# A fused attention and expert stage on Trainium2: a fifth place for the tanh arguments, and TensorE's side work cut and spread

## What is computed

```
def _L3_attn_ref(x, W1, b1, w2, b2):          # x normalised, h = 128 channels, A = 16
    f = x @ W1[:h]; g = x @ W1[h:]
    t = tanh(f[:, :, None, :] + g[:, None, :, :] + b1)     # every query against every key
    scores = einsum('bija,a->bij', t, w2[:, 0]) + b2[0]
    e = exp(scores) * tril(ones, -1)
    w = e / (sum(e, -1) + 1e-10)
    return einsum('bij,bjh->bih', w, x)

def _L3_ffn_ref(x, router_w, router_b, expert_w, expert_b):  # 8 experts, 2 chosen
    p = softmax(x @ router_w + router_b); top_p, top_i = top_k(p, 2)
    return sum over the two of top_p / sum(top_p) * (x @ expert_w[e] + expert_b[e])
...
t = t + attn(ln(t));  t = t + ffn(ln(t))
```

## Time and profile before

| what | value |
|---|---|
| device time, median of 3 runs | 8661.0 us (8649.36 to 8665.69) |
| the profiled execution's own time | 8667.4 us |
| its span in the profile | 8665.6 us |
| attention and expert stage: first tanh to last | 4323.9 to 8524.5 us |
| ScalarE over the whole span | busy 5504.1 us, 64% |
| granted TensorE clock, mean of the span | 0.91 |

### The profile page before, as it was taken

The page is one execution under the profiler, slowest core; times in us unless marked ns, Lnnn a source line. Parts: engine busy times, 40 slices in busy tenths (PEclk is TensorE's granted clock), DMA queues, the critical chain, the costliest instruction groups (busy, mean ns, idle before and its releaser), DMA issues. The chain is left out here.

```text
span 8665.6 us, 101771 instructions
## 1 busy us (share of the span) xinstructions
PE 6767.0 (78%) x37262; PEld 2438.1 (28%) x37262; DVE 6266.1 (72%) x12006; ACT 5504.1 (64%) x4244; POOL 1750.1 (20%) x1553
## 2 busy tenths in 40 slices
PE   8999999987887249966876766777867877678776
PEld 3333333323443113323322212222222222222222
DVE  6777777766764653347777777888878888789885
ACT  3222222213554342234499998999989999899995
POOL 5655666640000210004600000000000000000002
PEclk9999999997888569987999999999999999999998
DMA  1000000001010000000000000000000000000000
GB/s 47 1 1 1 1 1 1 1 4 25 23 25 8 7 0 0 0 0 3 8 1 1 1 1 1 1 1 1 10 1 1 1 1 11 1 1 1 1 11 13
DMA packets 24154, 46.13 MB, mean 5 GB/s; under 512 B 10394, under 2 KB 13596, under 8 KB 22558
## 3 DMA queue, kind: packets, MB, share of 16 engines
q1 hardware_dynamic: 23710, 40.17, 1.5%
HBM read 14.98 MB, written 8.39 MB: 3 GB/s over the span
## 5 line engine op out<-in xcount | busy, mean ns | idle before, releaser
L2437 ACT ACTIVATE aa_tanh<-aa_tanh 128x4096 f32<-128x4096 f32 (+8 forms) x1280 | 3692.4, 2952 | 261.0 <-DVE aa_tanh L2608 260.6
L2608 DVE TENSOR_SCALAR aa_tanh<-aa_f_times,aa_g_bias 128x1024 f32<-128x1024 f32 (+18 forms) x5120 | 2984.3, 644 | 705.3 <-PE aa_scores L2481 701.2
L2481 PE MATMUL aa_scores<-aa_tanh,aa_w_spread 128*32 128x512 f32 (+8 forms) x18432 | 2164.9, 587 | 836.2 <-ACT aa_tanh L2437 833.5
L2481 PEld LDWEIGHTS aa_scores<-aa_tanh,aa_w_spread 128*32 128x32 f32 x18432 | 609.6, 112 | 2233.5 <-ACT aa_tanh L2437 1179.8
L278 POOL TENSOR_TENSOR near_tap_weights<-near_hat_y_mask,near_hat_x 128x1024 f32<-128x1024 f32 x400 | 937.4, 2364 | 475.4 <-PE near_weights_spread L570 466.8
L584 PE MATMUL near_out_sum<-near_weighted,near_w_out 128*128 128x512 f32 x1984 | 1001.1, 628 | 24.0 <-DVE near_weighted L357 13.5
L570 PE MATMUL near_weights_spread<-near_tap_weights,near_spread_consts 36*64 36x512 f32 x6272 | 801.0, 611 | 19.0 <-DVE near_weighted L357 12.9
L2495 PE MATMUL aa_out_sum<-aa_weights,aa_normed 128*128 128x512 f32 (+3 forms) x1152 | 615.1, 657 | 185.1 <-DVE aa_weights L2617 185.1
L346 DVE TENSOR_TENSOR near_weighted<-near_weights_spread,near_values 128x1024 f32<-128x1024 f32 x496 | 589.4, 1220 | 154.8 <-PE near_weights_spread L570 154.7
L346 DVE TENSOR_TENSOR near_weights_spread<-near_weights_spread,near_values 128x1024 f32<-128x1024 f32 x288 | 353.9, 1229 | 342.4 <-PE near_weights_spread L570 342.4
L2404 POOL TENSOR_SCALAR aa_group_normed<-x_rows,norm_scale,aa_shift_plus 128x128 f32<-128x128 f32 x96 | 78.5, 830 | 2476.6 <-PE aa_turned L2521 1742.0
(11 more groups left out here) (372 smaller groups left out, 7233.1 us busy)
## 6 DMA issues: line engine op xcount, KB each, us to landing
l_taps<-l_scan_in_out SPq DMA_DIRECT2D x256, 64.0 KB, 2.0
x_rows<-in_x SPq DMA_DIRECT2D x4, 2048.0 KB, 14.3
out_x<-x_rows SPq DMA_DIRECT2D x4, 2048.0 KB, 6.3
qa_x<-in_L_attn_w SPq DMA_DIRECT2D x1, 1024.0 KB, 5.5
L_ffn_expert_w<-in_L_ffn_expert_w SPq DMA_DIRECT2D x2, 512.0 KB
near_spread_consts<-in_deform_consts SPq DMA_DIRECT2D x1, 805.5 KB, 7.8
aa_weights_in<-in_attention SPq DMA_DIRECT2D x1, 577.5 KB
l_weights<-in_mamba SPq DMA_DIRECT2D x1, 557.0 KB
```

Of the source, the lines that this page charges most:

```text
L2437: a.activation(TH[:, tt, 0:length], TH[:, tt, 0:length], ACT.Tanh).then_inc(th_ready, 1)
L2481: last = t.matmul(sp_[32 * q:32 * q + 32, n % 2, s:e], W2S[:, tt, :], TH[:, tt, o + s:o + e], start=tt == 0, stop=tt == 3, tile_position=( ...
L2608: ins = v.tensor_scalar(TH[:, tt, at[q]:at[q] + w - s], FR[:, m % 2, lo + s:CHUNK], GB[:, key:key + 1], None, ALU.add)
```

## The change

- TH gets five places instead of four; slot k uses place k mod 5 (`PLACES`). VectorE's half of a side job comes five slots after TensorE's, an expert's additions six.
- `add_tile` is cut: the first 512 columns are added after slot 3's scores of the next tile, the second 512 after slot 0's scores of the tile after that. The wait for the mask stands in front of both halves.
- `mask` moves on VectorE from after slot 2's fill to after slot 3's, and `keep_out` from slot (2, 0) to (2, 1).
- The expert side work uses slots 0 to 2 of full tiles that carry no job of the chunk's own, up to the chunk's end (113 to 116 positions in an image, of which 105 are used; before 124 positions in four-slot tiles).
- `keys` uses four column groups of 32 with 32-column stationary operands, two matmuls to a group, eight in all; the DMA of weights shrinks from 1155 to 195 columns.
- `out_T` shares its buffer with `normed_T`, and the experts' raw weights are loaded into `group_T`.

```diff
-AW = 8 * P + P + 3
+AW = 2 * 32 + P + 3
...
-    keys = np.zeros((P, 8, 8, 16), np.float32)
-    for j in range(8):
+    keys = np.zeros((P, 2, 2, 16), np.float32)
+    for j in range(2):
...
+PLACES = 5
...
-        TH = sb("tanh", [P, 4, 4 * CHUNK])
+        TH = sb("tanh", [P, PLACES, 4 * CHUNK])
...
-        OT = sb("out_T", [P, CHUNK])
+        OT = UT
...
-            at = [(n, tt) for n, (m, j) in enumerate(tiles) for tt in range(4)
-                  if m // NCH == b + 1 and j < m % NCH * CT_ and 4 <= n - first_of[m] < (m % NCH + 1) * CT_ - 5]
+            at = [(n, tt) for n, (m, j) in enumerate(tiles) for tt in range(3)
+                  if m // NCH == b + 1 and j < m % NCH * CT_ and n - first_of[m] >= 4 and own_job(n, tt) is None]
...
-        added = {(n + 1 + (tt == 3), (tt + 1) % 4): x[1] for (n, tt), x in behind.items() if x[0] == "e"}
+        added = {divmod(4 * n + tt + PLACES + 1, 4): x[1] for (n, tt), x in behind.items() if x[0] == "e"}
...
             def keys(m):
                 t.wait_ge(*bank_before("g", m))
-                for j in range(8):
-                    last = t.matmul(bank("g", m)[:, 0:P], WG[:, j, :], UT[:, j:CHUNK:8], start=j == 0, stop=j == 7)
+                for j in (0, 2, 4, 6, 1, 3, 5, 7):
+                    r = j // 2 * 32
+                    last = t.matmul(bank("g", m)[r:r + 32, 0:P], WG[:, j % 2, :], UT[:, j:CHUNK:8], start=j % 2 == 0, stop=j % 2 == 1, tile_position=(0, r))
...
-            def add_tile(n):
+            def add_half(n, h):
+
                 m, j, diagonal, lo, w = shape(n)
                 if diagonal:
                     t.wait_ge(masked, 1 + diagonals[n])
                 else:
                     t.wait_ge(e_ready, 1 + n + 1)
-                if j == 0 and m:
+                if j == 0 and m and not h:
                     t.wait_ge(ot_ready, 1 + m)
-                for h in range(2):
-                    s0 = max(lo, h * BANK)
-                    if s0 < (h + 1) * BANK:
...
-                last.then_inc(o_done, 1)
+                s0 = max(lo, h * BANK)
+                if s0 < (h + 1) * BANK:
...
+                    if h:
+                        last.then_inc(o_done, 1)
...
                     if tt == 3 and n:
-                        add_tile(n - 1)
+                        add_half(n - 1, 0)
+                    elif tt == 0 and n >= 2:
+                        add_half(n - 2, 1)
...
-                if n:
-                    v.wait_ge(th_used, 1 + 4 * (n - 1) + tt + 1)
+                if 4 * n + tt >= PLACES:
+                    v.wait_ge(th_used, 1 + 4 * n + tt - PLACES + 1)
...
-                    if n >= 2 and tt == 2:
+                    if n >= 2 and tt == 3:
                         mask(n - 2)
-                    if m and (i, tt) == (2, 0):
+                    if m and (i, tt) == (2, 1):
                         keep_out(m - 1)
-                    if not n:
+                    if 4 * n + tt < PLACES:
                         continue
-                    name, at = own_job(n - 1, tt) or (None, 0)
+                    slot = divmod(4 * n + tt - PLACES, 4)
+                    name, at = own_job(*slot) or (None, 0)
```

More of the change, by code:

```diff
@@ L2222, in attention_rows @@
     b2 = np.broadcast_to(np.asarray(w["b2"], np.float32).reshape(1, 1), (P, 1))
-    return np.ascontiguousarray(np.concatenate([keys.reshape(P, 8 * P), np.tile(w1[:h], (1, 8))] + tile8 + [b2], axis=1))
+    return np.ascontiguousarray(np.concatenate([keys.reshape(P, 64), np.tile(w1[:h], (1, 8))] + tile8 + [b2], axis=1))
 GE = 4 * EX
 STEPS, PERIOD = 18, 11
+PLACES = 5
 NGI = NT // 4
@@ L2255, in attention_and_experts @@
         W = sb("weights_in", [P, AW])
-        WG = W[:, 0:8 * P].rearrange("p (j c) -> p j c", c=P)
-        WF, B1C, W2C, B2C = W[:, 8 * P:9 * P], W[:, 9 * P:9 * P + 1], W[:, 9 * P + 1:9 * P + 2], W[:, 9 * P + 2:9 * P + 3]
+        WG = W[:, 0:64].rearrange("p (j c) -> p j c", c=32)
+        WF, B1C, W2C, B2C = W[:, 64:64 + P], W[:, 64 + P:65 + P], W[:, 65 + P:66 + P], W[:, 66 + P:67 + P]
         UN, UT, FR = sb("normed", [P, L]), sb("normed_T", [P, CHUNK]), sb("f_8_times", [P, 2, CHUNK])
         GB = sb("g_bias", [P, L // 8])
-        TH = sb("tanh", [P, 4, 4 * CHUNK])
+        TH = sb("tanh", [P, PLACES, 4 * CHUNK])
         ET = sb("weights", [P, 2, CHUNK])
-        OT = sb("out_T", [P, CHUNK])
+        OT = UT
         SHA, ST4 = sb("attention_shift_plus_1", [P, TT]), sb("sums_stats", [P, 24])
@@ L2266, in attention_and_experts @@
         EWC, RWC, RB, CM = sb("expert_w_centred", [P, EX, P]), sb("router_w_centred", [P, EX]), sb("router_in", [P, 2, EX]), sb("centring", [P, P])
-        EW, EB = OT, FR[:, 1, :]
         MU, MT, SH1 = sb("group_normed", [P, BANK]), sb("group_T", [P, 2, BANK]), sb("shift_plus_1", [P, NT])
+        EW, EB = MT[:, :, :].rearrange("p a n -> p (a n)"), FR[:, 1, :]
         LG, S1, S2 = (sb(n, [P, GE]) for n in ("logits", "first", "second"))
@@ L2375, in _ @@
             sp.dma_start(W[:, :], d["attention"]).then_inc(loaded, 16)
-            for dst, a, b in ((EW[:, :], 0, EX * P), (EB, EX * P, 2 * EX * P), (RB[:, :, :].rearrange("p a e -> p (a e)"), 2 * EX * P, 2 * EX * P + 2 * EX)):
+            for dst, a, b in ((EW, 0, EX * P), (EB, EX * P, 2 * EX * P), (RB[:, :, :].rearrange("p a e -> p (a e)"), 2 * EX * P, 2 * EX * P + 2 * EX)):
                 sp.dma_start(dst, d["experts3"][:, a:b]).then_inc(loaded_e, 16)
@@ L2436, in _ @@
                     a.wait_ge(sum_ready, 1 + 4 * n + tt + 1)
-                    a.activation(TH[:, tt, 0:length], TH[:, tt, 0:length], ACT.Tanh).then_inc(th_ready, 1)
+                    a.activation(TH[:, (4 * n + tt) % PLACES, 0:length], TH[:, (4 * n + tt) % PLACES, 0:length], ACT.Tanh).then_inc(th_ready, 1)
                     if n and tt == (2 if w >= BANK else 3):
@@ L2480, in scores @@
                         o = at[q] - 32 * q * diagonal
-                        last = t.matmul(sp_[32 * q:32 * q + 32, n % 2, s:e], W2S[:, tt, :], TH[:, tt, o + s:o + e], start=tt == 0, stop=tt == 3, tile_position=(0, 32 * q))
+                        last = t.matmul(sp_[32 * q:32 * q + 32, n % 2, s:e], W2S[:, tt, :], TH[:, (4 * n + tt) % PLACES, o + s:o + e], start=tt == 0, stop=tt == 3, tile_position=(0, 32 * q))
                 last.then_inc(th_used, 1)
-            def add_tile(n):
+            def add_half(n, h):
                 m, j, diagonal, lo, w = shape(n)
@@ L2489, in add_tile @@
                     t.wait_ge(e_ready, 1 + n + 1)
-                if j == 0 and m:
+                if j == 0 and m and not h:
                     t.wait_ge(ot_ready, 1 + m)
-                for h in range(2):
-                    s0 = max(lo, h * BANK)
-                    if s0 < (h + 1) * BANK:
-                        last = t.matmul(op[:, s0:(h + 1) * BANK], UN[:, j * P:(j + 1) * P], ET[:, n % 2, s0 - lo:(h + 1) * BANK - lo], start=j == 0, stop=n == closes(m, h))
-                last.then_inc(o_done, 1)
+                s0 = max(lo, h * BANK)
+                if s0 < (h + 1) * BANK:
+                    last = t.matmul(op[:, s0:(h + 1) * BANK], UN[:, j * P:(j + 1) * P], ET[:, n % 2, s0 - lo:(h + 1) * BANK - lo], start=j == 0, stop=n == closes(m, h))
+                    if h:
+                        last.then_inc(o_done, 1)
             def turn_out(m, h):
@@ L2577, in _ @@
                         turn_back(at)
-            add_tile(len(tiles) - 1)
+            add_half(len(tiles) - 2, 1)
+            for h in range(2):
+                add_half(len(tiles) - 1, h)
             for h in range(2):
@@ L2607, in fill @@
                     key = 16 * j + 4 * q + tt
-                    ins = v.tensor_scalar(TH[:, tt, at[q]:at[q] + w - s], FR[:, m % 2, lo + s:CHUNK], GB[:, key:key + 1], None, ALU.add)
+                    ins = v.tensor_scalar(TH[:, (4 * n + tt) % PLACES, at[q]:at[q] + w - s], FR[:, m % 2, lo + s:CHUNK], GB[:, key:key + 1], None, ALU.add)
                     if q == 3:
@@ L2763, in _ @@
                         keep_router()
-                    name, at = behind.get((n - 1, tt), (None, 0))
+                    name, at = behind.get(slot, (None, 0))
                     if name == "mt":
@@ L2770, in _ @@
                         keep_back(at)
-                    G, steps = choose.get((n - 1, tt), (0, ()))
+                    G, steps = choose.get(slot, (0, ()))
                     for step in steps:
```

## The result

The changed kernel takes 8536.0 us (median of 4 runs, 8524.1 to 8538.7) against 8659.7 before: ratio 0.9856, 95% interval 0.9839 to 0.9873, 124 us less. Forecast were 8515 and 8460 to 8605.

What follows compares the result with a forecast made beforehand. ScalarE was taken to bound the attention stage, losing 261 us in a ring short of room at certain places. Gains 3.3 + 112 + 24 + 7 = 146 us gave 8515 us against the median, range 8460 to 8605.

Steps and rivals of the forecast that it cites:

- Start: Before the first tanh: shorter keys' projection gains 3.0 us and the smaller DMA 0.3, together 3.3.
- Chunks with full tiles: Twelve chunks with full tiles: of 171 us ScalarE idle time 59 remain, a gain of 112.
- Chunks 4, 8, 12 and 0: Chunks of diagonal tiles alone: 8 us gained in each of 4, 8, 12 (24), and 7 in chunk 0.
- the mask holds TensorE as before: Middle of chunks 4, 8, 12: the 3.4 us wait stays, leaving 3.7 us gained there.
- Mask, cost 0: Mask one fill (2.73 us) later on VectorE costs nothing, as a fill may run one place further ahead.
- Rival A: The mask's wait replaces the ring's: 70 TensorE waits each grow 2.73 us, slower at 8706; 3 in 100.
- Halves, cost 0: Weighted sums cut in two on TensorE: no work added, covered by the gap before slot 3's scores, cost 0.
- a gain where ScalarE is short of places: Halved sums: without cover, 1.2 us of TensorE moves to the next slot, which helps where places are short.
- Positions: Expert work beside full tiles: three positions need 15.3 us of VectorE, four 16.7; 10 us left for uneven spread.
- Rival B: VectorE bounds where ScalarE stalls; a fifth place only moves stalls, gain about 60 us: 8600; 14 in 100.
- Rival D: Layout changes cost TensorE 0.3 us each, two more in 320 tiles; gain falls to 70, 8591; 4 in 100.
- room in the ring: Attention stage: engines wait round a ring short of room at certain places; ring or order can gain 261 us at most.

Runs made afterwards that it cites:

- experiment 3: The changed kernel, five places kept, with the mask moved back to after slot 2's fill: 8507 us, ratio 0.9825.
- the last kernel: Changed kernel with mask after slot 2's fill, another order of diagonal tiles, and no mask or exponent wait in first halves without columns: 8487 us, ratio 0.9801.
- the other order: The changed kernel with the eight diagonal tiles of place-0 chunks reordered, so VectorE's out jobs fall beside a 768-wide tile: 8516 us, ratio 0.9834.

## Why the prediction was right, and where it was not

The time, the sign and the mechanism of the whole were right: the tanhs' busy time stayed, and ScalarE's wait for sums fell from 260.6 to 119 (about 115 was named). The time fell by less than that wait, since ScalarE now also stands 12.5 us for scores and 3.9 us more for the gating, which the sum did not have. That the total came out is in part luck: one term was 18 us too large, another 7 too small. By parts:

- *Start*, 3.3 forecast: from the end of the step that makes `norm_shift`, just ahead of the stage, to the first tanh it is 19.1 us instead of 22.6, 3.5 less. VectorE's wait for the keys went from 3.03 to 0.40, and the projection took 1.14 us where 1.0 was taken. ScalarE's wait before the first tanh is 15.96 where 14.3 was named.
- *Chunks with full tiles*, 112 forecast: 20.2 + 35.4 + 30.8 + 32.4 = 119, of which 112 are idle time and the rest busy time that is a little shorter. The idle time that is left, 59, is the forecast's to the microsecond, but not its parts: 36 for sums where 46 was left, 17 for the gating where 13 was, and 7 for scores where nothing was. The 1.6 us that arithmetic left behind each 128-wide tile is 1.66 in the trace, and the 3.7 of place-1 chunks is 2.8.
- *Chunks 4, 8, 12 and 0*, 24 + 7 forecast: 6.1 + 0.8 + 4.6 and 1.3, 13 in all. This is the term that was mis-sized, and it accounts for the missing time. The sum credited the second half of chunks 4, 8 and 12 with 4.5 us each; in chunk 4 ScalarE's stalls there fell from 8.0 to 6.0, by 2. What failed is the step "the mask holds TensorE as before": a fill later, it takes back on TensorE what the fifth place gives. Undoing it gives 25.6 us in these four chunks (experiment 3), which makes 39 where 31 was forecast. The stalls at the two out jobs, 5.1 and 5.0 us, remain.
- *Mask, cost 0*: false. It costs 29 us with five places (21 in the stage) and 239 with four. Rival A had the mechanism right; it was given 3 in 100 because five places hold the wait beside full tiles, and there it is indeed hidden: chunks of place 1 and 2 are as long with the early mask as without. It was missed that in chunks of narrow tiles alone five places hold too little to cover it.
- *Halves, cost 0*: right with five places (1 us, inside the noise). In a ring of four they gain 48, as the step "a gain where ScalarE is short of places" has it.
- *Positions*, counted inside the 112: 11 us in five places (17 in the stage).
- Rival B (VectorE the bound) is out for the whole, since far more than its 60 us came, and for the place-0 chunks' total by the order of tiles. At the out jobs its sign is there all the same: VectorE works from 5358.3 us on without a gap while ScalarE stalls 5.1 and 5.0 us.
- Rival D is refuted by whole sums costing the same as halves. It counted two more changes of layout in each of 320 tiles; the traces show fewer, 1581 changes between 128*32 and 128*128 records with halves against 1351 with whole sums and 1249 in the kernel before, and nothing is seen of the 230 in the time. The Trainium skill's rule that changing the tiling mode drains the TensorE ("TensorEngine Tiling (Array Packing)", Key Properties) has no price here that a run could show.

What the forecast did not see is how the gain is shared. It put the whole under "room in the ring". The runs show two sets that each bring some 100 of the 124 us: five places and the keys, with the late mask (96), or halves, positions and keys in four places, with the early mask (99). The keys alone, 24, are in both. Beyond them the stage is 81 us shorter with the first set, 78 with the second and 129 with all and the early mask, so that the two overlap by some 30 us or more, as the first set still has the late mask. That they cure some of the same stalls is the likely reason; no trace was read stall by stall for it. The late mask then takes 21 to 29 back. The merged buffers and the smaller DMA were never undone alone. Undoing one part at a time from the changed kernel would have read "halves 1, positions 11, places 260": none of these is what the part contributes.

Left open: the remaining wait for sums, 79.7 us in the last kernel, was not taken apart, nor what the other order gives in chunk 0.

## What to carry to other kernels

In a ring of engines with strict queues, a step that one engine waits for belongs as early in its maker's queue as its inputs allow; moved one item later it is cheap only while the ring has a spare place (21 to 29 us with it here, 239 without), so test the two together and apart. Measure parts of a change both by taking one away and by adding one, since parts that cure the same stall look worthless one way and decisive the other. Try long side jobs beside wide slots: beside narrow ones the same work can stall the engine that sets the time, though the sum of work says that it fits. And judge a small edit by the length of the stage that it touches: a median of the whole launch also holds what the edit never touched.

## What was not expected of the hardware

The keys' projection, 16 records of 128 columns with a stride of eight elements in the moving operand, runs 3.5 times as fast in four column groups with 32-column stationary operands: 1.11 us against 3.97, both at a granted clock of 1.00, although each record still lasts 0.41. Records overlap, then. Two things changed at once, the groups and the width of what is loaded: the 16 weight loads fill 3.2 us of the old projection and 0.54 of the new one at the start. No run tells which of the two set the old pace. And a long wait costs TensorE once more: after standing 8.2 us for a mask its next 16 score records took 3.50 us at a granted clock of 0.54 (near the lower level, 1.2 GHz), the same records a few us later 1.92 at 1.00 (2.4 GHz). It is no single case: after each of the 16 times that TensorE stood over 6 us in this stage of the changed kernel, and each of the 8 in the kernel before, the granted clock was 0.50 for the next 2.5 us. The rows (windows of the changed kernel, columns as above; the last is one of the others):

```profile
5594.80:5598.20 3.40, 3.40 (x17) 0.57 (x17) 2.52 (x4) 3.40 (x3) 0.00 (x0) 0.54 0.00 0
5599.70:5601.50 1.80, 1.80 (x18) 0.36 (x17) 1.34 (x3) 1.80 (x2) 0.00 (x0) 1.00 0.00 0
5586.50:5594.70 8.20, 0.00 (x0) 0.00 (x0) 8.20 (x15) 8.15 (x3) 0.00 (x0) 0.78 0.00 0
5418.70:5421.20 2.50, 2.50 (x14) 0.96 (x18) 2.50 (x4) 2.46 (x4) 0.00 (x0) 0.50 0.03 7
```
